# Five of sixteen scan inputs made by ScalarE and TensorE, and the softplus of the step sizes ordered by channel group

## The reference, cut to what matters

```
xs   = the convolved image in 4 directions             # [4, 192, 1024] per image
dts, Bs, Cs = split(x_proj(xs))                        # 24 + 16 + 16 rows
delta = softplus(dt_proj(dts) + bias)                  # [4, 192, 1024]
for each direction, state n and channel:
    h[t] = exp(delta[t] * A[n]) * h[t-1] + (delta[t] * u[t]) * B[n, t]
    y[t] = sum over n of h[t] * C[n, t]
```

## Time and profile before

| | |
|---|---|
| timed runs, median (lowest to highest) | 2042.33 us (2037.89 to 2042.62) |
| the profiled execution | 2036.25 us |
| its span | 2034.4 us |
| granted TensorE clock, mean of the span | 0.858 |
| VectorE busy | 1546.7 us (76%) |
| TensorE busy | 1529.8 us (75%) |
| GpSimd busy | 1368.0 us (67%) |
| ScalarE busy | 847.2 us (42%) |

### The profile page before, as it was taken

How to read it: one execution, slowest core, us unless ns; L and a number is a source line. 1 busy time by engine, 2 the same in 40 slices (tenths; PEclk the granted TensorE clock), 3 DMA queues, 4 the chain that set the end, 5 groups by cost and what they waited for, 6 DMA issues and landing times.

```text
span 2034.4 us, 14482 instructions
## 1 busy us (share of the span) xinstructions
PE 1529.8 (75%) x3788; PEld 675.1 (33%) x3789; DVE 1546.7 (76%) x1634; ACT 847.2 (42%) x1288; POOL 1368.0 (67%) x517
## 2 busy tenths in 40 slices
PE   5855677676777676996477777777777586999997
PEld 2312232232232232632122222222223253555554
DVE  5459999997999997545799999999999673322322
ACT  3664544544545543266454444554454411111110
POOL 2438998997999993033699999999999402222231
PEclk9857888897888888796688888898888887999999
DMA  3173345346344321204634534434433482111110
GB/s 111 69 269 147 127 137 165 125 133 190 114 142 144 116 97 62 86 37 179 223 124 141 171 112 141 144 116 139 144 113 113 145 291 77 40 48 46 47 50 17
DMA packets 120144, 248.91 MB, mean 122 GB/s; under 512 B 20863, under 2 KB 33698, under 8 KB 116241
## 3 DMA queue, kind: packets, MB, share of 16 engines
q1 hardware_dynamic: 114960, 234.00, 34.7%
q0 software_dynamic: 5120, 14.21, 2.3%
HBM read 205.10 MB, written 44.60 MB: 123 GB/s over the span
## 4 chain that ended last, share of the span: by engine, by line
DVE 37%; PE 28%; POOL 11%; issue 9%; DMA 7%; ACT 4%; SPq 3%; POOLq 0%; DVEq 0%
DVE arena L834 22%; PE psum L1211 9%; POOL arena L450 9%; DVE arena L821 8%; DMA arena<-bc_dram 7%; PE psum L1230 5%; PE psum L1056 3%; PE psum L1086 3%; SPq L328 3%; POOL arena L435 2%; PE psum L1109 1%; PE psum L1071 1%; DVE psum L805 1%; DVE arena L809 1%; DVE arena L804 1%
## 5 line engine op out<-in xcount | busy, mean ns | idle before, releaser
L1109 PE MATMUL psum<-arena,ident 128*128 128x512 f32 x1536 | 819.2, 688 | 290.0 <-POOL arena L450 289.2
L450 POOL TENSOR_TENSOR arena<-arena 128x1536 f32<-128x1536 f32 x256 | 875.0, 3438 | 74.7 <-DMA arena<-bc_dram 36.4
L834 DVE TENSOR_TENSOR_SCAN arena<-psum,arena 128x512 f32<-128x512 f32 x768 | 897.2, 1227 | 14.5 <-ACT psum L637 14.4
L637 ACT ACTIVATE psum<-arena 128x512 f32<-128x512 f32 x768 | 528.4, 691 | 621.3 <-DVE arena L834 621.3
L1109 PEld LDWEIGHTS psum<-arena,ident 128*128 128x128 f32 x1536 | 323.9, 219 | 782.0 <-POOL arena L450 415.3
L821 DVE TENSOR_TENSOR arena<-psum,arena 128x1536 f32<-128x1536 f32 x176 | 304.3, 1729 | 25.8 <-issue 20.7
L435 POOL TENSOR_TENSOR arena<-arena 128x1536 f32<-128x1536 f32 x80 | 275.1, 3439 | 0.1
L1211 PE MATMUL psum<-arena 128*128 x480 | 203.7, 561 | 0.0
L425 POOL TENSOR_TENSOR arena<-arena 128x1024 f32<-128x1024 f32 x24 | 70.7, 2945 | 126.5 <-DVE arena L809 126.5
L487 POOL TENSOR_TENSOR gap<-one 128x1 f32<-128x1 f32 x40 | 11.3, 283 | 211.9 <-DVE arena L998 211.9
L711 ACT ACTIVATE arena<-psum 128x384 f32<-128x384 f32 x40 | 19.6, 490 | 301.6 <-PE psum L1202 301.6
(11 more groups left out here) (149 smaller groups left out, 1150.0 us busy)
## 6 DMA issues: line engine op xcount, KB each, us to landing
arena<-bc_dram SPq DMA_DIRECT2D x1024, 128.0 KB, 3.0
step_dram<-arena SPq DMA_DIRECT2D x16, 1536.0 KB, 6.6
arena<-step_dram SPq DMA_DIRECT2D x32, 768.0 KB, 8.2
arena<-in_x SPq DMA_DIRECT2D x8, 1536.0 KB, 8.8
arena<-in_w SPq DMA_DIRECT2D x6, 1876.0 KB, 10.7
t_dram<-arena SPq DMA_DIRECT2D x16, 386.0 KB, 4.1
arena<-in_w SPq DMA_DIRECT2D x4, 1536.0 KB, 14.2
z_dram<-arena SPq DMA_DIRECT2D x2, 1536.0 KB, 5.4
```

The lines of the kernel that those rows point to most:

```text
L450: g.tensor_tensor(x, x, Cs[c % C_RING][:, None, :].to_broadcast([P, CG, HALF]), ALU.mult)\
L637: a.activation(dA[e % 2], steps[g % 2][0][:, j, :], ACT.Exp, scale=A[:, KORDER[kk], j, n:n + 1]).then_inc(s_dA, 1)
L834: v.tensor_tensor_scan(x, dA[(CG * c + j) % 2][:, ::way], x, 0.0 if first else state[:, n, j:j + 1], ALU.mult, ALU.add)\
L1109: ins = pe.matmul(bank[j], ident[:, :], X3[c % RING][:, j, :], start=False, stop=(n == NS - 1), skip_group_check=True)
```

## The change

Of 16 states, 4 inputs are now made by GpSimd (P), 7 by VectorE (D) and 5 by ScalarE (A), in the order of `MAKER`. For an A step, du stands transposed in SBUF (`duT`, tokens on the partitions, one copy out of psum per group). B(n) is then one number per partition, so ScalarE scales duT in 8 blocks of 128 x 3 x 64 (`scale_duT`), placed in the steps by the table `SCALED`. TensorE transposes the result into the two psum banks that hold the decay in other steps (`transpose_input`), and the decay of an A step goes to SBUF (`dAs`) instead. The scan reads its input from psum and writes the ring slot. The columns of B come from xd by TensorE transposes and a ScalarE copy (`b_columns`). TensorE's `add_up` runs two steps behind the step counter. B rows are loaded 5 steps ahead, none for A steps.

In the softplus stage ScalarE works channel group by channel group (Abs, the logs of the group before, Exp), and `xd_out` moves from ScalarE to VectorE. x of the next pair is loaded after the scans (its place in SBUF now holds duT and the scaled blocks), `norm_stats` of the next pair goes behind `times_z`, and `norm_std` behind the layer norm's scaling.

```diff
-BY_GPSIMD = (1, 4, 7, 10, 13)
+MAKER = "PDADPDADPDADPDAA"
+BY_SCALAR = (2, 6, 10, 14, 15)
+LAST_D = 13
+SCALED = {15: ((2, 0, 3),), 0: ((2, 3, 8),), 2: ((6, 0, 2),), 4: ((6, 2, 8),), 6: ((10, 0, 5),),
+          8: ((10, 5, 8), (14, 0, 3)), 10: ((14, 3, 8),), 12: ((15, 0, 6),), 13: ((15, 6, 8),)}
+LAG = 2
+B_AHEAD = 5
+LB = HALF // P
...
+        duT = arena[:, 0:CG * HALF]
+        scaled = [arena[:, (1 + u) * CG * HALF:(2 + u) * CG * HALF] for u in range(2)]
+        blocks = lambda ap: ap.rearrange("p (j t b c) -> p j t b c", j=CG, t=LB, b=2)
+        dAs = [arena[:, 3 * CG * HALF + j * HALF:3 * CG * HALF + (j + 1) * HALF] for j in range(CG)]
...
-                    if s + B_RING < STEPS:
-                        load_b(s + B_RING)
+                    if s + B_AHEAD < STEPS and MAKER[(s + B_AHEAD) % NS] != "A":
+                        load_b(s + B_AHEAD)
...
                     if s == 4 * NS and p + 1 < PAIRS:
-                        load_x(p + 1)
+                        sp.dma_start(win, w_in).then_inc(s_win, 16)
                 sp.wait_ge(s_scan, CG * STEPS * (p + 1))
+                if p + 1 < PAIRS:
+                    load_x(p + 1)
...
-                    if s + 2 < STEPS and (s + 2) % NS in BY_GPSIMD:
+                    if s == 0:
+                        input_of(0)
+                    if s + 2 < STEPS and MAKER[(s + 2) % NS] == "P":
                         input_of(s + 2)
-                    if s == 0 and 1 in BY_GPSIMD:
-                        input_of(1)
...
+                def b_columns(i):
+                    c, cols = ND * p + i, bank[0].rearrange("p (t b n) -> p t b n", t=TT, b=4)[:, :, 0:2, :]
+                    a.wait_ge(s_btps, c + 1)
+                    a.activation(BT[:, PREP[i], :, :, 0:4], cols[:, :, :, 2:15:4], ACT.Copy)
+                    a.activation(BT[:, PREP[i], :, :, 4], cols[:, :, :, 15], ACT.Copy).then_inc(s_bt, 1)
                 if p:
                     a.wait_ge(s_tst, 16 * 2 * GROUPS)
-                xd_out(0)
...
+                def logs(n):
+                    j, par = (n - 1) % CG, (n - 1) // CG % 2
+                    e = g3(E[par])[:, j, :]
+                    a.wait_ge(s_e, n)
+                    if n > CG * ND * p + CG:
+                        a.wait_ge(s_delta, n - CG)
+                    a.activation(g3(one_e)[:, j, :], e, ACT.Identity, bias=one[:, :]).then_inc(s_u, 1)
+                    a.activation(g3(ln_e)[:, j, :], e, ACT.Ln, bias=one[:, :]).then_inc(s_ln, 1)
                 for i in range(ND):
-                    c, par = ND * p + i, i % 2
-                    E3 = g3(E[par])
-                    if i >= 2:
-                        a.wait_ge(s_delta, CG * (c - 1))
+                    E3 = g3(E[i % 2])
+                    if i:
+                        b_columns(i)
                     for j in range(CG):
-                        a.wait_ge(s_vps, CG * c + j + 1)
+                        n = CG * (ND * p + i) + j + 1
+                        if i >= 2:
+                            a.wait_ge(s_delta, n - 2 * CG)
+                        a.wait_ge(s_vps, n)
                         a.activation(E3[:, j, :], V3[j], ACT.Abs).then_inc(s_abs, 1)
-                    if 0 < i < ND - 1:
-                        xd_out(i + 1)
-                    for j in range(CG):
-                        a.wait_ge(s_abs, CG * c + j + 1)
+                        if i or j:
+                            logs(n - 1)
+                        a.wait_ge(s_abs, n)
                         a.activation(E3[:, j, :], E3[:, j, :], ACT.Exp, scale=-1.0).then_inc(s_e, 1)
                     if i == 0:
-                        xd_out(1)
-                    for j in range(CG):
-                        n = CG * c + j + 1
-                        a.wait_ge(s_e, n)
-                        if i:
-                            a.wait_ge(s_delta, n - CG)
-                        a.activation(g3(one_e)[:, j, :], E3[:, j, :], ACT.Identity, bias=one[:, :]).then_inc(s_u, 1)
-                        a.activation(g3(ln_e)[:, j, :], E3[:, j, :], ACT.Ln, bias=one[:, :]).then_inc(s_ln, 1)
+                        b_columns(0)
+                logs(CG * ND * (p + 1))
+                def duT_out(g):
+                    a.wait_ge(s_duTps, GROUPS_OF_PAIR * p + g + 1)
+                    a.wait_ge(s_scaled, 2 * LB * inputs_before(STEPS * p + g * NS, "A"))
+                    a.activation(duT.rearrange("p (j l) -> p j l", j=CG), dups, ACT.Copy).then_inc(s_duT, 1)
+                def scale_duT(s, first, last):
+                    kk, g, half, n, _ = place(s)
+                    c = STEPS * p + s
+                    index = inputs_before(c, "A")
+                    a.wait_ge(s_duT, GROUPS_OF_PAIR * p + g + 1)
+                    a.wait_ge(s_bt, ND * (p + 1))
+                    if index >= 2:
+                        a.wait_ge(s_inT, CG * (index - 1))
+                    for t in range(first, last):
+                        k, b = t // 2, t % 2
+                        a.activation(blocks(scaled[index % 2])[:, :, k, b, :], blocks(duT)[:, :, k, b, :], ACT.Copy,
+                                     scale=BT[:, kk, LB * half + k, b, BY_SCALAR.index(n):BY_SCALAR.index(n) + 1])\
+                         .then_inc(s_scaled, 1)
                 def du_to_psum(g):
                     a.wait_ge(s_steps[g % 2], 32 * (GROUPS_OF_PAIR // 2 * p + g // 2 + 1))
-                    if p or g:
-                        a.wait_ge(s_dbv, inputs_before(STEPS * p + g * NS, False))
+                    a.wait_ge(s_duT, GROUPS_OF_PAIR * p + g + 1)
                     a.activation(dups, steps[g % 2][1], ACT.Copy).then_inc(s_dups, 1)
                 def exp(s, j):
                     kk, g, _, n, _ = place(s)
-                    e = CG * (STEPS * p + s) + j
+                    c = STEPS * p + s
+                    e = CG * c + j
+                    if MAKER[n] == "A":
+                        if inputs_before(c, "A"):
+                            last = max(q for q in range(c) if MAKER[q % NS] == "A")
+                            a.wait_ge(s_scan, CG * last + j + 1)
+                        a.activation(dAs[j], steps[g % 2][0][:, j, :], ACT.Exp,
+                                     scale=A[:, KORDER[kk], j, n:n + 1]).then_inc(s_dAs, 1)
+                        return
...
+                    todo = [(g * NS + m if m > n else (g + 1) * NS + m, f, l) for m, f, l in SCALED.get(n, ())]
+                    exp(s, 0)
+                    exp(s, 1)
                     if s == 0:
+                        duT_out(0)
                         du_to_psum(0)
+                        scale_duT(BY_SCALAR[0], 0, 3)
+                    if s and place(s - 1)[4]:
+                        keep_state(s - 1)
+                    if MAKER[n] == "A" or n % 2:
+                        exp(s, 2)
                     if n == NS - 1 and g + 1 < GROUPS_OF_PAIR:
                         du_to_psum(g + 1)
-                    exp(s, 0)
-                    exp(s, 1)
-                    if s and place(s - 1)[4]:
-                        keep_state(s - 1)
-                    exp(s, 2)
+                    for m, f, l in todo:
+                        if m < STEPS:
+                            scale_duT(m, f, l)
                     if n == 2 and g:
                         y_out(g - 1)
+                    if not (MAKER[n] == "A" or n % 2):
+                        exp(s, 2)
+                    if n == NS - 2 and g + 1 < GROUPS_OF_PAIR:
+                        duT_out(g + 1)
...
+                def xd_out(i):
+                    c = ND * p + i
+                    if i >= 2:
+                        v.wait_ge(s_vps, CG * (c - 1))
+                        v.wait_ge(s_bcst[i - 2], 16 * (p + 1))
+                    for h in range(2):
+                        v.wait_ge(s_xdps, 2 * c + h + 1)
+                        v.tensor_scalar(xd[i % 2][:, h * HALF:(h + 1) * HALF], bank[h], brow, None, ALU.add)\
+                         .then_inc(s_xd, 1)
                 v.wait_ge(s_xcr, CG * (p + 1))
+                xd_out(0)
...
+                        if j == 0 and i + 1 < ND:
+                            xd_out(i + 1)
...
+                        x, ring = X3[c % RING][:, j, ::way], dA[(CG * c + j) % 2][:, ::way]
+                        if maker == "A":
+                            count = CG * inputs_before(c, "A") + j + 1
+                            v.wait_ge(s_dAs, count)
+                            v.wait_ge(s_inT, count)
+                            decay, given = dAs[j][:, ::way], ring
+                        else:
+                            v.wait_ge(s_dA, CG * rows_before(c) + j + 1)
+                            decay, given = ring, x
+                        v.tensor_tensor_scan(x, decay, given, 0.0 if first else state[:, n, j:j + 1],
+                                             ALU.mult, ALU.add).then_inc(s_scan, 1)
...
                 times_z(0)
                 times_z(1)
+                if p + 1 < PAIRS:
```

(53 more changed lines are left out.)

75 lines of the change are left out of this document (36 added, 39 removed).

## The result

| | before | after |
|---|---|---|
| median of the runs | 2041.57 us (2037.89 to 2042.62, 4 runs) | 1971.97 us (1967.72 to 1974.22, 4 runs) |
| profiled execution, span | 2036.25, 2034.4 us | 1967.72, 1965.9 us |
| mean granted clock | 0.858 | 0.908 |

The account below looks back on a forecast made before the run. VectorE was taken to bound the scans, 1207 of 2034 us, with GpSimd close behind. Scans -73, softplus and start +19, norm_stats +6: -48 us, 1988 profiled, 1994 us forecast for the timed runs; range 1943 to 2042.

Parts of the forecast that it names:

- What VectorE loses, four products a group, and 66.6 us of work: Scan stage: VectorE sheds 6.6 us a group, leaving 7 products and 16 steps of scans, 66.6 us.
- The gaps before steps 14 and 2 as laid out, 2.6 us; 69.2 in all: Scan stage: VectorE waits for TensorE's banks, 2.1 us at step 14 and 0.5 at step 2; group 69.2 us.
- The bound passes to GpSimd.: Scan stage: GpSimd's 20 operations, 67.8 us a group, become the bound, 7.6 us below the old period.
- Half a slow add_up a group on the path, 1.3 us: Scan stage, TensorE: about one add_up in seven slow, half of one on the path; group 70.5 us, bounds 67.8 and 76.
- 3 us a pair for the first step and the tail: Scan stages: 3 us a pair added to 16 groups of 70.5 us, 1134 us against 1207.
- The softplus stage and the start, +19: Before the scans: last delta 6 us later through a longer chain, start 3.4 us longer; 9.4 a pair, +19 us.
- norm_stats, +6: Between the pairs: the second pair's statistics move to where VectorE idles only 1.61 us; +6 us.
- Scalings at 0.35 us, ScalarE no bound: Scan stage: 40 scalings at 0.35 us each, 14 us a group; ScalarE busy 54 of 68 us.
- TensorE at its low clock (2088): Rival, scan stage: half-clock add_ups behind transposes make TensorE the bound, 76.4 us a group, 2088 us; chance 0.15.
- GpSimd's bound with a free softplus order (1946): Rival: scan stages reach GpSimd's bound, 68.3 us a group, and the softplus order costs nothing; 1946 us; chance 0.15.
- The gain eaten by the rest (2026 to 2052): Rival: scans gain only 25 to 41 us, 25 to 35 lost outside them; 2026 to 2052 us; chance 0.12.

Follow-up runs that it names:

- experiment 5: Changed kernel with the input of state 4 made by VectorE instead of GpSimd: 1992.06 us, ratio 0.9751 to the kernel before.
- experiment 4: Changed kernel with TensorE's 12 transposes of du ahead of add_up(11) instead of behind it: 1957.46 us, ratio 0.9577 to the kernel before.
- experiment 6: Changed kernel with one transpose per bank of an A step instead of four, three quarters of these inputs stale: 1969.25 us, ratio 0.9633 to the kernel before.
- experiment 8: Changed kernel with du transposes ahead of add_up(11), reordered softplus queues, and norm_stats of the second pair's first image ahead of the layer norm: 1921.72 us.
- experiment 7: Changed kernel with softplus queues reordered: xd_rows(i+1) behind two channel groups' dt matmuls, B columns, logs and xd_out(1) moved: 1943.74 us, ratio 0.9524 to the kernel before.
- experiment 2: Kernel before with only the softplus order changed (ScalarE by channel group, xd_out on VectorE), no B columns: 2029.11 us, ratio 0.9934.
- experiment 3: Changed kernel with the softplus stage in its old order, xd_out on ScalarE, B columns kept: 1980.58 us, ratio 0.9695 to the kernel before.

## Why the prediction was right, and where it was off

It said 1994 us and a group of 70.5 us; the time was 1972 and the group 69.1. The mechanism was right: VectorE sheds four products a group, and giving it one back (experiment 5) costs about that product again, 14 us a stage. One term of the sum was mis-sized, the slow add_ups. By its own steps:

- *What VectorE loses, four products a group, and 66.6 us of work.* Right: 533.3 us busy in each stage is 66.7 a group. The 3.44 us a step were read across a group border, six scans of which three belong to an odd and three to an even group; that this gave the mean of 3.53 and 3.35 was luck.
- *The gaps before steps 14 and 2 as laid out, 2.6 us; 69.2 in all.* Right in sum and place: a stage of 552.9 us is 69.1 a group, 2.4 over VectorE's work, mostly before step 14 behind add_up(11) and the transposes of du, as said. It is not spread as laid out (3.2 and 1.1 in turn where 2.1 was said, nearly none before step 2); as both values are waits, their mean is near the one laid out for a group of mean length. Experiment 4 showed the order on TensorE to be the cause of the odd groups' wait and of a part of the even groups'; the rest is GpSimd's backlog and, in some groups, a slow add_up.
- *"The bound passes to GpSimd."* Not borne out for the changed kernel, though 539.1 us busy was near the 542 said. Taking an input from GpSimd did not remove the waits (experiment 5). VectorE and the gaps set the period, which is also how the 69.2 was laid out. It became true with experiment 4's order, in its second pair: 68.2 us a group.
- *Half a slow add_up a group on the path, 1.3 us.* This is the term that was mis-sized: 16 x 1.3 = 21 of the 28.7 us by which the scans came out shorter than forecast. The share of slow add_ups was carried over from the kernel before, though the change fills the idle times after which they came. The clock granted in the stages rose from 0.85 to 0.95, and an add_up averages 2.80 us. Even at 2.98 in experiment 6 the stage was no longer (with transposes gone, so that is no clean price). What stays of the term can be read before step 14: in four of the 16 groups add_up(10) and (11) take 7.0 to 7.1 us together instead of 6.2, which is 0.2 us a group at most where 1.3 was said. The place was right all the same: in experiment 8, with seven slow ones, the scan stages are no shorter than here in spite of the better order.
- *3 us a pair for the first step and the tail.* Wrong place. Within the scans nothing of it shows; but two A steps at the end leave four add_ups behind their transposes, 4.6 us after the first pair and the 3.6 after the second (VectorE's wait there is 15.84 us for 12.17). In sum 8 where 6 was allowed.
- *The softplus stage and the start, +19.* Right: 5.0 and 3.5 us in pair one (said 6 and 3.4), and 21.1 - 4.6 - 5.7 = 10.8 in pair two, as what is left over. The terms of the chain add up to 20.5 to 23.7 us, not the 22 to 25 written; the trace has 24.0 from the first delta of direction 1 to that of direction 2. The chain was the named one, and experiment 7 took it away. But "the new order" was not the loss: experiments 2 and 3 show it to be a gain of 9 to 14 us, the B columns and the place of xd_rows being what costs.
- *norm_stats, +6.* Right, 5.7 us: 9.2 for the two, less the 1.61 of waiting and the 1.9 of rows ready early.
- *Scalings at 0.35 us, ScalarE no bound.* Right: six take 2.17 us and five 1.82, so 0.35 each from start to start, and ScalarE is busy for 407 of 553.

So -101.7 in the scans where -73 was forecast, and +33.2 outside where +25 was.

The rivals. TensorE at its low clock (2088) did not occur: the trace shows the upper level of 2.4 GHz even in a stretch whose matmuls are transposes but for the last 0.6 us:

```profile
233.00:238.50 5.50, 3.13 (x19) 2.11 (x19) 5.50 (x6) 4.39 (x7) 5.50 (x3) 1.00 0.33 113
```

The rows show the clock rising within transposes, and experiment 6 shows it falling when transposes are left out. With this the rule of the Trainium skill ("TensorE: Matmul & The Clock Gate", Part 4), that the fast clock does not engage for transpose mode, does not agree; the measurements decide. GpSimd's bound with a free softplus order (1946) needed both halves, and neither came in the changed kernel. The gain eaten by the rest (2026 to 2052) had the right places, but a third of the scans' gain, not most, was what they cost.

## What to carry to other kernels

When work moves to an idle engine, do not carry its share of slow instructions over: here they came after its idle times, and the added work filled these. Ask instead which few instructions on the path still start after a pause (here add_up(10)). Look at more than one stretch of a periodic stage before taking a duration from it: here every second group was 2.8 us longer. Lay out the queue order around the added steps, for that gave the period to 0.2 us, and read from it which one instruction to move; here such moves (experiments 4, 7, 8) brought another 50 us, where the change itself had brought 70. Before moving an instruction ahead in a queue, look whether the engine has a pause there: where it has none, only what is behind it gets later.

## What the runs showed of the hardware

An operation of VectorE with both inputs in SBUF stood still beside GpSimd's. GpSimd's timeline, then VectorE's, in the changed kernel:

```profile
109.12 2.35 POOL L446 TENSOR_TENSOR arena<-arena 128x1024 f32<-128x1024 f32 x1 [8.39 <-DVE arena L877]
```
```profile
105.29 1.22 DVE L872 SCALAR_TENSOR_TENSOR arena<-arena 128x1024 f32<-128x1024 f32 x1 [6.99 <-ACT arena L624]
...
109.22 3.33 DVE L872 SCALAR_TENSOR_TENSOR arena<-arena 128x1024 f32<-128x1024 f32 x1 [0.18 <-ACT arena L624]
112.59 1.23 DVE L873 SCALAR_TENSOR_TENSOR psum<-psum,arena 128x1024 f32<-128x1024 f32 x1
```

Begun 0.10 us after GpSimd's product, it took 3.33 us instead of 1.22 and ended 1.08 after GpSimd's end at 111.47: it seems to have waited for the whole of the other. In the kernel before the turn was the other way: GpSimd's product took 3.23 us in the median of 24 instead of the 2.35 of the earlier trace rows. The scans and products of the scan stage have an operand in psum and take 1.23 and 1.73 us on average beside a GpSimd that is hardly idle. With this agrees the Trainium skill, "SBUF — State Buffer", Who interferes with whom: the pair of ports that the two share is an exclusive lock, and a VectorE instruction with two SBUF inputs contends for it.
